# The top-2 layer's answers are added inside the feature attention's pipeline

## The reference

```python
# layer 2: top-2 mixture of experts
probs = softmax(layernorm(x) @ router_w)
expert_gate, expert_index = top_k(probs, 2)
v, y = selected(wv * sv), gelu(selected(w * s))
out = sum(expert_gate * selected(v * y, w1 * s1), over the 2 picks)
x = x + out
# layer 3: attention by random features (16 heads of 8)
q, k, v = heads(layernorm(x) @ W.T + b)
qp, kp = exp(td - diag - max) + EPS          # td = (t * dn) @ proj.T; max per token for q, over all for k
out = (qp @ (kp.T @ v)) / (qp @ sum(kp))
x = x + relu((out @ Wo.T + bo) @ Wfc.T + bfc)
```

## Time and profile before

| | |
|---|---|
| median of 3 runs | 3237.78 us (3218.44, 3237.78, 3242.75) |
| the profiled execution, its own time | 3219.48 us |
| its span in the trace | 3217.3 us |
| busy in the span | PE 88%, DVE 51%, ACT 47%, POOL 43% |
| top-2 layer's answers, first issue to last add | 554.98 to 575.26 us |
| feature attention | 576.36 to about 722.4 us |

### The profile page before, as it was taken

How to read it: one execution, slowest core, us unless ns; L and a number is a source line. 1 busy time by engine, 2 the same in 40 slices (tenths; PEclk the granted TensorE clock), 3 DMA queues, 4 the chain that set the end, 5 groups by cost and what they waited for, 6 DMA issues and landing times. The chain is left out here.

```text
span 3217.3 us, 45570 instructions
## 1 busy us (share of the span) xinstructions
PE 2840.9 (88%) x14432; PEld 1780.3 (55%) x14432; DVE 1656.8 (51%) x4065; ACT 1525.0 (47%) x3103; POOL 1389.3 (43%) x1281
## 2 busy tenths in 40 slices
PE   6886997796758989876989999999999998999998
PEld 4565886675743433345974444444444444677776
DVE  4436333655238999975325555555555555211111
ACT  3431222432548787731325566666556664344443
POOL 0012665423629999953434555555555554000000
PEclk9898999897878999997989999999999999899999
DMA  5002655201112222324000000000000000000000
GB/s 169 0 27 77 177 172 157 89 1 36 43 55 80 73 80 76 78 76 162 26 12 1 1 0 0 0 0 0 0 0 0 0 1 1 16 11 7 13 7 26
DMA packets 90748, 140.46 MB, mean 44 GB/s; under 512 B 12211, under 2 KB 47942, under 8 KB 90614
## 3 DMA queue, kind: packets, MB, share of 16 engines
q1 hardware_dynamic: 80502, 118.41, 12.1%
q0 software_dynamic: 9728, 19.94, 2.4%
q10 hardware_dynamic: 384, 0.46, 0.1%
HBM read 122.19 MB, written 24.97 MB: 46 GB/s over the span
## 5 line engine op out<-in xcount | busy, mean ns | idle before, releaser
L1731 POOL TENSOR_TENSOR l3a_p<-l3a_p,l3a_rden 128x512 f32<-128x512 f32 x512 | 521.6, 1040 | 482.1 <-DVE l3a_rden L1767 479.3
L1757 DVE CUSTOM_DVE_ANT_0 l3a_p<-bank,relative_bias 128x512 f32<-128x512 f32 x512 | 333.5, 689 | 213.6 <-PE bank L1906 206.7
L1827 ACT ACTIVATE l3a_p<-l3a_p,l3a_low 128x512 f32<-128x512 f32 x512 | 365.4, 719 | 4.6 <-DVE l3a_low L1757 4.6
L1915 PEld LDWEIGHTS bank<-ident,l3a_p 128*128 128x128 f32 x2048 | 228.4, 140 | 162.7 <-issue 158.1
L2648 POOL TENSOR_TENSOR l2a_dBu<-l2a_du,l2a_bs 128x1024 f32<-128x1024 f32 x128 | 299.2, 2351 | 35.2 <-DVE l2a_h L2872 33.8
L1833 ACT COPY l3a_pT<-bank 128x512 f32<-128x512 f32 x256 | 150.2, 587 | 324.2 <-PE bank L1915 323.8
L2872 DVE TENSOR_TENSOR_SCAN l2a_h<-bank,l2a_dBu 128x1024 f32<-128x1024 f32 x128 | 290.2, 2278 | 8.7 <-ACT bank L2779 8.7
L1906 PE MATMUL bank<-l3a_kT,l3a_qT 64*128 64x512 f32 x1024 | 291.0, 645 | 1.4 <-DVE l3a_low L1757 0.7
L881 DVE SCALAR_TENSOR_TENSOR x<-bank,l3f_gates,x 128x128 f32 x256 | 85.5, 351 | 371.8 <-PE bank L909 371.8
L1915 PE MATMUL bank<-ident,l3a_p 128*128 128x128 f32 x2048 | 273.6, 276 | 0.6 <-ACT l3a_pT L1833 0.5
L909 PEld LDWEIGHTS bank<-l3fe_w,l3fe_h 128*128 128x128 f32 x2048 | 233.7, 192 | 15.3 <-issue 15.3
(11 more groups left out here) (515 smaller groups left out, 4866.4 us busy)
## 6 DMA issues: line engine op xcount, KB each, us to landing
l2a_bs<-l2a_b_rows SPq DMA_DIRECT2D x128, 256.0 KB, 3.3
l0fe_wi<-in_L_ffn_in_dram SPq DMA_DIRECT2D x40, 516.0 KB
l0fe_wo<-in_L_ffn_out_dram SPq DMA_DIRECT2D x40, 320.0 KB
by_place<-by_distance SPq DMA_DIRECT2D x16, 512.0 KB, 14.8
relative_bias<-by_place SPq DMA_DIRECT2D x16, 448.0 KB, 11.8
l0fe_answers<-l0f_y_rows SPq DMA_DIRECT2D x16, 256.0 KB, 5.1
l3fe_w<-in_L_ffn_W_dram SPq DMA_DIRECT2D x16, 256.0 KB
switch_out<-in_L_ffn_out_dram SPq DMA_DIRECT2D x1, 2560.0 KB, 14.3
```

What stands on the lines that cost most here:

```text
L1731: ins = pool.tensor_tensor(a, a, rden[:, t, h:h + 1].to_broadcast([P, S]), ALU.mult)
L1757: bk.drain(dve.tensor_tensor_reduce(p[u % 2][h][:, t, :], ps(job)[:], bias[:, u % HP * 2 + h, b0:b0 + S], 1.0, 3.0e38, ALU.add, ALU.min, l ...
L1827: ins = act.activation(a, a, ACT.Exp, bias=low[h][:, t:t + 1], scale=-1.0, accum_out=den[:, t, h:h + 1])
L1915: ins = pe.transpose(ps(job)[:, t * P:(t + 1) * P], p[u % 2][h][:, t, kt * P:(kt + 1) * P], chip.ident[:])
```

## The change

The top-2 layer's block ends when SP has issued the 16 loads of the answers; nobody in it waits for them. The tile for the answers, their gates and eight semaphores (one for each sequence) move into an object `Answers` that lives until the end of the feature attention. There DVE adds the answers of sequence `q` directly ahead of `statistics(q)`: the first pick's 4 tiles, then the second's, each tile with one `scalar_tensor_tensor` that multiplies by the gates; ACT's multiplications and DVE's adds of 512 columns are gone. The small `memset` of ones in `v` moves ahead of the first statistics.

```diff
+class Answers:
+    def load(self, sp, y_rows):
+        for q in range(B):
+            for k in range(self.top):
+                at = 1 + k * NT * P + q * S
+                sp.dma_start(self.rows[:, k, q * TPS:(q + 1) * TPS, :], y_rows[at:at + S, :].rearrange("(t p) d -> p t d", p=P)).then_inc(self.loaded[q], 16)
+
+    def add(self, chip, dve, chain, q):
+        dve.wait_ge(self.loaded[q], 16 * self.top)
+        for k in range(self.top):
+            for n in range(q * TPS, (q + 1) * TPS):
+                ins = dve.scalar_tensor_tensor(chip.x[:, n, :], self.rows[:, k, n, :], self.gates[:, k, n:n + 1], chip.x[:, n, :], ALU.mult, ALU.add)
+            chain.link(ins)
...
@@ block_experts
-                for i in range(B):
-                    for k in range(top):
-                        at = 1 + k * NT * P + i * S
-                        sp.dma_start(answers[:, k, i * TPS:(i + 1) * TPS, :],
-                                     y_rows[at:at + S, :].rearrange("(t p) d -> p t d", p=P)).then_inc(answered[i], 16)
+                answers.load(sp, y_rows)
...
-                if top > 1:
-                    for i in range(B):
-                        act.wait_ge(answered[i], 16 * top)
-                        for t in range(TPS):
-                            n = i * TPS + t
-                            ins = act.mul(answers[:, 1, n, :], answers[:, 1, n, :], pick_gates[:, 1, n:n + 1])
-                        ins.then_inc(scaled, 1)
...
-                order = Chain(dve, add_order)
-                for i in range(B):
-                    dve.wait_ge(answered[i], 16 * top)
-                    for t in range(TPS):
-                        n = i * TPS + t
-                        ins = dve.scalar_tensor_tensor(chip.x[:, n, :], answers[:, 0, n, :], pick_gates[:, 0, n:n + 1],
-                                                       chip.x[:, n, :], ALU.mult, ALU.add)
-                    if top > 1:
-                        order.link(ins)
-                        dve.wait_ge(scaled, i + 1)
-                        xs_ = chip.x[:, i * TPS:(i + 1) * TPS, :]
-                        dve.tensor_tensor(xs_, xs_, answers[:, 1, i * TPS:(i + 1) * TPS, :], ALU.add)
...
@@ feature_attention
                 dve.memset(minus_half[:], -0.5).then_inc(minus_half_ready, 1)
-                statistics(0)
                 for u in range(2):
                     ins = dve.memset(v[u][:, :, :, DC:], 1.0)
                 ins.then_inc(ones_ready, 1)
-                for q in range(1, AHEAD):
+                for q in range(AHEAD):
+                    answers.add(chip, dve, c, q)
                     statistics(q)
...
                     if i + AHEAD < B:
+                        answers.add(chip, dve, c, i + AHEAD)
                         statistics(i + AHEAD)
```

More of the change, by code:

```diff
@@ L608, in bcast, with route @@
     return ap2.rearrange("p (m o) -> p m o", o=1).to_broadcast([ap2.shape[0], m, n_after])
-def route(chip, ctx, L, NR, bias, top=None, capacity=None, threshold=False, b2=None, load_behind=None):
+def route(chip, ctx, L, NR, bias, top=None, pick_gates=None, capacity=None, threshold=False, b2=None, load_behind=None):
     nc = chip.nc
@@ L619, in route @@
     picks = [chip.sb(ctx, f"{L}_pick{k}", [P, NT, E8]) for k in range(top or 0)]
-    pick_gates = chip.sb(ctx, f"{L}_pick_gates", [P, top, NT]) if top else None
+    if top and pick_gates is None:
+        pick_gates = chip.sb(ctx, f"{L}_pick_gates", [P, top, NT])
     if capacity:
@@ L911, in _, with __init__ @@
                                 bk.fill(ins, ("y", u))
+class Answers:
+    def __init__(self, chip, ctx, name, top, rows=None):
+        self.top = top
+        self.rows = chip.sb(ctx, f"{name}_answers", [P, top, NT, D]) if rows is None else rows
+        self.gates = chip.sb(ctx, f"{name}_answer_gates", [P, top, NT])
+        self.loaded = [chip.nc.alloc_semaphore(name=f"{name}_answers_loaded{q}") for q in range(B)]
+    def load(self, sp, y_rows):
[9 more added lines that the diff above has]
+            chain.link(ins)
 GB = 2 * P
@@ L1029, in place, with block_experts @@
     return expert, source, target
-def block_experts(chip, L, top, xn_rows, y_rows, expert, source, target, pick_gates, w_in, w_out, act_fn, glu):
+def block_experts(chip, L, top, xn_rows, y_rows, expert, source, target, answers, w_in, w_out, act_fn, glu):
     nc = chip.nc
@@ L1047, in block_experts @@
         g = each(2, "g", [P, J, GB]) if glu else h
-        answers = sb("answers", [P, top, NT, D])
         warm = sb("warm", [P, 1])
@@ L1052, in block_experts @@
         fetched, sent = [sem(f"fetched{u}") for u in range(NX)], [sem(f"sent{u}") for u in range(NY)]
-        answered = [sem(f"answered{i}") for i in range(B)]
         xT_turned, xT_ready, h_summed, g_ready, v_summed, h_ready, y_summed, y_ready = (
             sem(n) for n in ("xT_turned", "xT_ready", "h_summed", "g_ready", "v_summed", "h_ready", "y_summed", "y_ready"))
-        scaled, add_order = sem("answers_scaled"), sem("add_order")
         hidden_ready = h_ready if glu else g_ready
@@ L1212, in _, with top2_glu_experts @@
                 answer(NB - 1)
-def top2_glu_experts(chip, w):
+def top2_glu_experts(chip, w, answers):
     L = "l0f"
@@ L1221, in top2_glu_experts @@
             normalise_and_route(chip, first, L, w["router_w"], turned_out=False, rows_out=xn_rows)
-        _, picks, pick_gates = route(chip, ctx, L, E8, None, top=2)
+        picks = route(chip, ctx, L, E8, None, top=2, pick_gates=answers.gates)[1]
         expert, source, target = place(chip, ctx, L, 2, picks, GB)
-        block_experts(chip, L, 2, xn_rows, y_rows, expert, source, target, pick_gates, w["in"], w["out"], ACT.Gelu_apprx_tanh, True)
+        block_experts(chip, L, 2, xn_rows, y_rows, expert, source, target, answers, w["in"], w["out"], ACT.Gelu_apprx_tanh, True)
 class SwitchWeights:
@@ L2056, in prepare, with feature_attention @@
         pool.tensor_scalar(self.scaled_bias[:, 1:2], self.bk, float(DH1) ** -0.25, 0.0, ALU.mult, ALU.add).then_inc(self.prepared, 1)
-def feature_attention(chip, held, experts):
+def feature_attention(chip, held, experts, answers):
     nc = chip.nc
@@ L3067, in build @@
             elif layer is feature_attention:
-                layer(chip, features, experts)
+                layer(chip, features, experts, top2_answers)
                 earlier.close()
+            elif layer is top2_glu_experts:
+                top2_answers = Answers(chip, earlier, "l0f", 2)
+                layer(chip, part(prefix), top2_answers)
             elif layer is switch_experts:
```

## The result

| | before | after |
|---|---|---|
| median | 3240.27 us (14 runs, 3218.44 to 3251.46) | 3258.50 us (14 runs, 3247.82 to 3269.09) |
| the profiled execution's span | 3217.3 us | 3253.3 us |

The ratio is 1.0061, 95% interval 1.0041 to 1.0081: the changed kernel is slower by about 18 us, clearly outside the noise and within 1%. The two spans differ by more (36.0 us), but 9.2 of that arose ahead of the change: the last scatter of the top-2 layer ended at 553.69 in one trace and at 562.87 in the other. From there to the first statistics of the switch layer it is 169.8 us before and 192.8 after, +23.0. The remaining 3.8 us lie behind it (the switch layer alone +5.1, 211.4 us against 206.3), in code that the change leaves alone; a later trace of the kernel before (before_third) has 211.9 us for that layer, so this part needs no cause in the change.

A forecast was written before the change was run, and what follows sets the result against it. DVE's adds bound the top-2 layer's end; PE bounds the attention rounds, with DVE's margin at `cx` 0.07 us. Seam -3, round 0 +2.9, rounds 1 to 4 +13.6 give +13.5 on 3230: about 3243 us, range 3214 to 3262.

The forecast's parts named there:

- the forecast case: Top-2 layer's end and feature attention: DVE's adds meet POOL and delay `cx`; +13.5 us in all, chance 0.42.
- the rival with a chance of 0.17: Feature-attention rounds: POOL gets in after each add and PE falls to half clock in some; +29 us, 3259, chance 0.17.
- the seam: From top-2 layer's end to feature attention's start: block ends with SP's last load issue; -3 us, -5.4 without contention.
- the 3230 I took: Baseline for the whole kernel before: middle of four shown times, 3218.44 to 3242.75, to which +13.5 was added.
- it waits for one group of four adds: Before the loop, POOL's `normalise(0)` meets `add(1)` and waits 1.14 us, within 1.9 us of contention on the path.
- Rounds 1 to 4, cx: DVE between `shift` and `cx`: adds and POOL alternate in groups of four adds, `cx` comes 3.5 us late each round.
- Rounds 1 to 4, length: Feature-attention rounds 1 to 4: about 18.2 us instead of 14.8, +3.4 a round, +13.6 for four.
- Round 0: Feature attention's first round: `add(3)` stands before the maxima of round 1; +2.9 us, +2.1 without contention.
- The rival without POOL: Seam and feature-attention rounds: the adds never meet POOL; +5 us, 3235, chance 0.27.
- the faster case: DVE between `shift` and `cx`: adds fill a wait for PE's `context` longer than 2.4 us; -5 us, 3225, chance 0.12.
- DVE's operation of 1.53 us in the earlier trace: Evidence for contention: a 128x512 DVE `tensor_tensor` took 0.69 us beside idle POOL, 1.53 beside working POOL, losing 0.84.

The follow-up runs named there:

- the second job: The changed kernel measured once more against the kernel before, beside other kernels on another chip: ratio 1.0083 (1.0062 to 1.0103).
- one_input: Changed kernel with eleven bn_stats reading one tensor in place of the eight adds in rounds 0 to 4; ratio to the kernel before 1.0039.
- before_again: The kernel before, unchanged, run once more for its trace on another chip; ratio 1 by definition, stage 176.4 us.

## Why the prediction was right

The forecast was +13.5 us; measured were +18 (interval 13 to 26) and, in the second job, +24 (20 to 33). The direction, the range and the place were right: the adds stand in front of `cx`, PE's `weigh` waits for it, and POOL makes the adds dearer. The size was too small, and in the rounds it was not the forecast case that happened but much of the rival with a chance of 0.17, finer turns and a falling clock. By its own signs the prediction said so: rounds of 18.2 us for the forecast and 20 for that rival (measured 20.2 and 19.7 on average), and it called itself wrong if PE's clock in the rounds fell well below 1.0, which it did (0.69 to 0.89). The rival's +29 was too much in three terms: the seam gave 4 us where it had 1, the lateness of `cx` came to 14.8 in four rounds where it had 20, and the clock to 4 where it had 6, since it falls in some rounds of the kernel before as well.

3243 was low by 5 us for the effect and by 10 because the kernel before has its median at 3240 in 14 runs, not at the 3230 I took; the range held both. That the rival's 3259 lies on the measured 3258.5 is an accident of that same 3230. Other chips gave 3165 for the kernel before, so it is the difference that counts. Step by step, with the means over the traces:

- *The seam.* The block started 1.19 us after SP's last issue, as said. From the last scatter to the maxima of round 0 it is 35.5 us before (36.8, 36.1, 33.7) and 31.5 after: -4.0, forecast -3. The first transposes came 8.2 us after the block's start: I had 7.8 without contention and 9.7 with it. The step "it waits for one group of four adds" was too dear: POOL's small operations lost 0.4 us in all. The four parts of the 8.2 are 0.41 to the first add (I had 0.15), 2.32 for the adds, 5.44 for statistics and POOL (5.05 and the 0.4 lost), and 0.05 to the transposes, where my 0.25 had no row behind it.
- *Rounds 1 to 4, cx.* Forecast 3.5 us late a round. Measured 4.0, 3.1, 3.4 and 4.2 in the first trace: right in size, in part by luck, since two errors cancel. The turns are those of the rival (one add between two operations of POOL, where I had four), so the block takes 3.1 to 4.8 us, not 3.4; in return `minus_mean` finds POOL idle (0.17 us) behind the blocks of 3.99 us and more, where I had it held, and is held (0.78) only behind the shorter ones (rounds 0 to 4 of two traces: five of ten).
- *Rounds 1 to 4, length.* Forecast 18.2 us, measured 20.2 and 19.7 on average. The term left out of the forecast's sum is the clock: I had put it into a rival. Rounds 1 to 4 cost 18.8 us more than before, for 13.6: 14.8 by the lateness of `cx` (the mean of both traces), and 4.0 by what the clock costs here beyond the 2.1 that it costs on average in the three traces of before.
- *Round 0.* 15.2 and 15.7 against 10.3, 13.1 and 13.1: +3.3, forecast +2.9.
- *The rest.* -0.8. The sum is about 17 us.

The rival without POOL (+5) was run as one_input, whose rounds were 17.1 as that case said, though its time was 12 us above before. In the rounds at full clock the faster case failed for the reason given: there is no wait in front of `cx`. In rounds at 0.90 there is one, also in the kernel before. This is its round 2 in before_again:

```profile
598.34 0.29 DVE L2169 TENSOR_TENSOR l1a_cx<-bank,feature_packed 128x128 f32<-128x128 f32 x1 [1.89 <-PE bank L2387]
```

There DVE waits 1.89 us for PE's `context`, less than the 2.4 that the case wanted; the prediction's rows of `cx` were all of a round without it.

One reading in it is off: DVE's operation of 1.53 us in the earlier trace rows lost 0.84, but the rest of POOL's operation at DVE's start was 0.99 (961.64 - 960.65). No step hangs on the difference.

## What to carry to other kernels

Before moving work into another stage's pipeline, look for the instruction behind it that the bounding engine waits for, not at the engine's busy share: DVE had 3.4 us idle in a round, and 2.3 us of work cost about 5 (3.8 to 6.6 in eight rounds, against those of before at full clock). Put such work where the engine already waits, and where GpSimd is idle if the work reads two tensors in SBUF. A one-line move took the loss from 0.6 to 0.8% to nothing measurable.

## What the hardware showed that was not expected

- DVE and POOL took turns instruction by instruction: one add of 0.35 us (0.26 to 0.27 from start to start) for each POOL operation of 1.04, for as long as both had work. POOL's operations of four columns held a run of adds up by nothing (2.31 us for eight) and lost up to 0.23 us each themselves.
- PE's clock was below 1.00 in rounds without any idle time in its records (16.40 of 16.40 us busy at 0.90, in the kernel before) as well as in those with 1.3 to 4 us of it (0.69 to 0.89, in the changed kernel), and at 1.00 in rounds with 2.07 us of it (one_input). With three unread matmuls in the gap it stood at 1.00 in two of four rounds.
- One kernel's stage varied between traces by 6.6 us (169.8 to 176.4), nearly all of it where the clock differs: rounds 0 to 2 +6.0, round 5 -1.7, from the maxima of round 7 on +2.9, and ahead of round 0 -0.6. A single pair of traces would have put the change at 12 to 23 us.
